# Layer 0's T1, M and output-bias products as three passes of split operands, and one load ring for x and transposed y

## What is computed

```python
q = Wq y + bq;  k = Wk y + bk;  v = Wv x + bv          # 8 heads of 32 channels
attn = softmax((q kT) / sqrt(256))                     # per head, 32 x 32
o = Wo (attn v) + bo + x
x1 = groupnorm over all channels and positions of o
```

## Time and profile before

| | |
|---|---|
| median of 3 runs | 1543.38 us (1541.15 to 1543.43) |
| the profiled execution | 1542.93 us, its span 1541.1 us |
| PE busy | 1511.2 us, 98% of the span |
| DVE busy | 1278.6 us, 83% |
| ACT busy | 1108.9 us, 72% |
| POOL busy | 450.8 us, 29% |
| granted TensorE clock, mean | 0.995 |

### The profile page before, as it was taken

The page is one execution under the profiler, slowest core; times in us unless marked ns, Lnnn a source line. Parts: engine busy times, 40 slices in busy tenths (PEclk is TensorE's granted clock), DMA queues, the critical chain, the costliest instruction groups (busy, mean ns, idle before and its releaser), DMA issues.

```text
span 1541.1 us, 54826 instructions
## 1 busy us (share of the span) xinstructions
PE 1511.2 (98%) x24146; PEld 1274.8 (83%) x24146; DVE 1278.6 (83%) x2024; ACT 1108.9 (72%) x2064; POOL 450.8 (29%) x294
## 2 busy tenths in 40 slices
PE   9999999999999999999999999999999999999995
PEld 6888888888888888888888888888888888888883
DVE  5778888888788887978879888888888889788897
ACT  6667676777767777677776776867767776777765
POOL 1114133141331413314142141422314133141321
PEclk9999999999999999999999999999999999999998
DMA  7232331423315233142422414233142331524212
GB/s 250 56 99 83 111 124 38 152 84 118 111 36 152 84 118 111 54 148 71 143 86 84 132 57 145 84 111 121 55 151 78 120 116 41 149 83 129 59 49 91
DMA packets 96397, 157.28 MB, mean 102 GB/s; under 512 B 5408, under 2 KB 38304, under 8 KB 96032
## 3 DMA queue, kind: packets, MB, share of 16 engines
q1 hardware_dynamic: 96160, 153.78, 31.8%
HBM read 120.20 MB, written 33.55 MB: 100 GB/s over the span
## 4 chain that ended last, share of the span: by engine, by line
PE 96%; DVE 1%; ACT 1%; issue 1%; POOL 0%; ACTq 0%; POOLq 0%; DVEq 0%
PE pj_ps L313 46%; PE l_ps L313 12%; PE s_ps L328 9%; PE w_ps L339 8%; PE l_ps L424 7%; PE w_ps L357 7%; PE l_ps L441 2%; PE l_ps L468 2%; PE l_ps L462 1%; PE l_ps L471 1%; PE s_ps L499 0%; PE l_ps L450 0%; DVE o_sb L972 0%; PE l_ps L432 0%; PE l_ps L489 0%
## 5 line engine op out<-in xcount | busy, mean ns | idle before, releaser
L1132 POOL TENSOR_TENSOR prob<-prob,row_inv 128x1024 f32<-128x1024 f32 x128 | 257.9, 2015 | 890.4 <-DVE row_inv L864 890.4
L671 ACT CAST att_hi<-w_ps 128x256 fp32r<-128x256 f32 x256 | 83.2, 380 | 192.2 <-PE w_ps L357 192.1
L313 PE MATMUL pj_ps<-y_hi,w_hi 128*128 128x512 f32 x510 | 207.4, 407 | 0.0
L313 PE MATMUL pj_ps<-y_hi,w_lo 128*128 128x512 f32 x510 | 202.0, 396 | 0.0
L313 PE MATMUL pj_ps<-y_lo,w_hi 128*128 128x512 f32 x510 | 202.0, 396 | 0.0
L859 DVE TENSOR_REDUCE row_sum<-prob 128x16 f32<-128x1024 f32 x128 | 155.0, 1211 | 49.2 <-ACT prob L640 49.1
L847 DVE TENSOR_REDUCE row_max<-s_ps 128x16 f32<-128x1024 f32 x128 | 155.6, 1215 | 21.2 <-PE s_ps L328 21.2
L328 PEld LDWEIGHTS s_ps<-k_s,q_s 32*64 32x64 f32 x8192 | 130.8, 133 | 43.1 <-issue 35.2
L1149 POOL TENSOR_TENSOR o_sb<-o_sb,u_sb 128x1024 f32<-128x1024 f32 x60 | 157.7, 2638 | 0.9
L854 DVE TENSOR_TENSOR prob<-s_ps,row_max 128x1024 f32<-128x1024 f32 x128 | 155.6, 1215 | 0.1
L635 ACT COPY prob_t<-w_ps 128x512 f32<-128x512 f32 x256 | 152.2, 596 | 3.8 <-PE w_ps L339 3.1
(11 more groups left out here) (139 smaller groups left out, 3552.2 us busy)
## 6 DMA issues: line engine op xcount, KB each, us to landing
y_raw<-in_ctx SPq DMA_DIRECT2D x64, 512.0 KB, 4.9
yt_raw<-in_ctx_t SPq DMA_DIRECT2D x64, 512.0 KB, 4.6
x_raw<-in_x SPq DMA_DIRECT2D x64, 512.0 KB, 5.1
out_z<-o_sb SPq DMA_DIRECT2D x60, 512.0 KB, 3.6
mask_b<-in_mask SPq DMA_DIRECT2D x64, 256.0 KB, 4.0
out_z<-o_sb SPq DMA_DIRECT2D x8, 256.0 KB, 2.7
u_sb<-in_w SPq DMA_DIRECT2D x2, 512.0 KB, 5.8
w_sb<-in_w SPq DMA_DIRECT2D x1, 1024.0 KB, 10.7
```

The source lines that it names most:

```text
L313: last = mm(dst, lhs, rhs, start=i == 0, stop=i == len(todo) - 1)
L1132: nc.gpsimd.tensor_tensor(cut, cut, row_inv[:, u % 2, :].unsqueeze(2).to_broadcast([P, 2 * HEADS, CHUNK]), ALU.mult).then_inc(probs_done, 1)
```

## The change

- Wk and Wv of layer 0 are split once into fp32r pairs (`w0_hi`, `w0_lo`), and bv into `bv_hl`. Wv is loaded into a part of u_sb. The ACT copies stand ahead of its loop, the DVE subtractions (`weights_low`) in slot 3 of the first sample.
- The Gram matrix is split in each sample: on ACT in slot 6 `split_upper` (two copies, 128x256 and 128x128) directly behind `copy_att`, and `split_lower` in the place of `copy_lower`; on DVE `gram_low` (three subtractions, 128x256, 128x128, 128x128) directly behind `sum_y`, which now signals `gram_done`.
- T1 is 2 x 2 three-pass products: 12 PE instructions of 256 columns in the place of 8.
- U is split: the ACT copy in slot 10 writes u_hi, and DVE's new `u0_low` (one 128x512 subtraction, slot 10, behind `split_y`) writes u_lo and signals `u0_copied`.
- M is 12 PE instructions of 256 columns in the place of 8, the bias product 8 of 2 columns in the place of 8 of 1; DVE adds the bias in two steps.
- Transposed y and x share two buffers. `load_yt` of the next sample's first two blocks moves to slots 14 and 15, `load_x` of the first two to slots 3 and 4.

```diff
-                if exists(n, 4, q - 2):
+                if q >= 4:
+                    sp.wait_ge(x_hi_done, count(n, 4, q - 2))
+                    sp.wait_ge(x_lo_done, count(n, 4, q - 2))
+                elif q >= 2:
                     sp.wait_ge(yt_hi_done, count(n, 4, q - 2))
...
-                    for start, load in ((S_SPLIT_T + 1, load_yt), (S_X + 1, load_x)):
...
+                    if s in (1, 2):
+                        load_yt(n, s + 1)
+                    if s in (3, 4):
+                        load_x(n, s - 3)
+                    if s - (S_X if last else S_X + 1) in (0, 1):
+                        load_x(n, s - (S_X if last else S_X + 1) + 2)
+                    if s in (14, 15) and not last:
+                        load_yt(n, s - 10)
@@ PE @@
                     for i in range(HALVES):
-                        for k in range(HALVES):
-                            last = mm(l0_ps[1][:, i * E:(i + 1) * E], gram[:, k, i * P:(i + 1) * P], w0_sb[:, K_W, k, :], start=k == 0, stop=k == 1)
+                        cut = slice(i * P, (i + 1) * P)
+                        last = three_pass(l0_ps[1][:, i * E:(i + 1) * E],
+                                          [((g_hi[:, k, cut], g_lo[:, k, cut]), (w0_hi[:, K0_SPLIT, k, :], w0_lo[:, K0_SPLIT, k, :])) for k in range(HALVES)])
...
                     for k in range(HALVES):
+                        cut = slice(k * P, (k + 1) * P)
+                        three_pass(l0_ps[0][:, k * E:(k + 1) * E],
+                                   [((w0_hi[:, V0_SPLIT, i, cut], w0_lo[:, V0_SPLIT, i, cut]), (u_hi[:, i, :], u_lo[:, i, :])) for i in range(HALVES)])
+                    for k in range(HALVES):
+                        cut = slice(k * P, (k + 1) * P)
                         for i in range(HALVES):
...
+                            mm(l0_ps[1][:, 2 * k:2 * k + 2], u_hi[:, i, cut], bv_hl[:, i, :], start=i == 0, stop=False)
+                            last = mm(l0_ps[1][:, 2 * k:2 * k + 2], u_lo[:, i, cut], bv_hl[:, i, :], start=False, stop=i == 1)
@@ ACT @@
+            def split_upper(n):
+                act.wait_ge(upper_done, count(n, 1, 0))
+                for i in range(HALVES):
+                    copy(g_hi[:, i, i * P:], gram[:, i, i * P:])
+
+            def split_lower(n):
                 act.wait_ge(lower_ready, count(n, 1, 0))
-                copy(gram[:, 1, 0:P], l0_ps[0][:, E:E + P]).then_inc(gram_done, 1)
+                copy(g_hi[:, 1, 0:P], l0_ps[0][:, E:E + P]).then_inc(gram_hi_done, 1)
...
                         copy_att(n, u - LAG)
+                    if s == S_SUM:
+                        split_upper(n)
                     if not first and s in (4, 6):
                         group_normed(n - 1, s // 2)
@@ DVE @@
+            def gram_low(n):
+                dve.wait_ge(gram_hi_done, count(n, 1, 0))
+                for i in range(HALVES):
+                    tt(g_lo[:, i, i * P:], gram[:, i, i * P:], g_hi[:, i, i * P:], ALU.subtract)
+                tt(g_lo[:, 1, 0:P], l0_ps[0][:, E:E + P], g_hi[:, 1, 0:P], ALU.subtract).then_inc(gram_done, 1)
+
+            def u0_low(n):
+                dve.wait_ge(u0_hi_done, count(n, 1, 0))
+                tt(u_lo[:, :, :], l0_ps[1][:, :].rearrange("p (i o) -> p i o", i=HALVES), u_hi[:, :, :], ALU.subtract).then_inc(u0_copied, 1)
...
                     if s == S_SUM:
                         sum_y(n)
+                        gram_low(n)
+                    if first and s == 3:
+                        weights_low()
...
+                    if s == S_U:
+                        u0_low(n)
```

More of the change, by code:

```diff
@@ L42 @@
 Q_W, K_W, V_W, O_W = range(4)
+Q0, K0, O0 = range(3)
+K0_SPLIT, V0_SPLIT = range(2)
 C_IDENT, C_HEAD, C_RESID, C_MEAN, C_NEG = 0, P, 2 * P, 2 * P + 2 * E, 3 * P + 2 * E
@@ L73, in build @@
         mean_mat = cst[:, C_MEAN:C_MEAN + P]
-        w0_sb = sb("w0_sb", [P, 4, HALVES, E])
+        w0_sb = sb("w0_sb", [P, 3, HALVES, E])
+        w0_hi = sb("w0_hi", [P, 2, HALVES, E], F32R)
+        w0_lo = sb("w0_lo", [P, 2, HALVES, E], F32R)
+        bv_hl = sb("bv_hl", [P, HALVES, 2], F32R)
         w1_hi = sb("w1_hi", [P, 4, HALVES, E], F32R)
@@ L121, in build @@
         o_bias = sb("o_bias", [P, HALVES])
+        o_part = sb("o_part", [P, HALVES])
+        g_hi, g_lo, u_hi, u_lo = m_hi, m_lo, m_hi, m_lo
         o_sb = sb("o_sb", [P, HALVES, L])
@@ L230, in load_x @@
             def load_x(n, q):
-                if exists(n, 4, q - 2):
+                if q >= 2:
                     sp.wait_ge(x_hi_done, count(n, 4, q - 2))
-                if exists(n, 4, q - 2):
                     sp.wait_ge(x_lo_done, count(n, 4, q - 2))
+                else:
+                    sp.wait_ge(yt_hi_done, count(n, 4, q + 2))
+                    sp.wait_ge(yt_lo_done, count(n, 4, q + 2))
                 sp.dma_start(x_raw[:, q % 2], x_d[n + q // 4][:, :, (q % 4) * BT:(q % 4 + 1) * BT]).then_inc(x_in[q % 2], 16)
@@ L449, in layer0 @@
                                 o = i * P + DH * h
-                                mm(l0_ps[0][DH * h:DH * h + DH, P + i * DH:P + (i + 1) * DH], y_sum_b[:, k, :], w0_sb[:, K_W, k, o:o + DH],
+                                mm(l0_ps[0][DH * h:DH * h + DH, P + i * DH:P + (i + 1) * DH], y_sum_b[:, k, :], w0_sb[:, K0, k, o:o + DH],
                                    start=k == 0, stop=k == 1)
@@ L455, in layer0 @@
                                 o = i * P + DH * h
-                                last = mm(l0_ps[0][DH * h:DH * h + DH, i * DH:(i + 1) * DH], w0_sb[:, Q_W, k, o:o + DH], t1[:, k, o:o + DH],
+                                last = mm(l0_ps[0][DH * h:DH * h + DH, i * DH:(i + 1) * DH], w0_sb[:, Q0, k, o:o + DH], t1[:, k, o:o + DH],
                                           start=k == 0, stop=k == 1)
@@ L461, in layer0 @@
                     for i in range(HALVES):
-                        last = mm(l0_ps[1][:, i * E:(i + 1) * E], a0_wide[:, i, :], w0_sb[:, O_W, i, :], start=True, stop=True)
+                        last = mm(l0_ps[1][:, i * E:(i + 1) * E], a0_wide[:, i, :], w0_sb[:, O0, i, :], start=True, stop=True)
                     last.then_inc(u0_ready, 1)
@@ L735, in _ @@
             last.then_inc(consts_done, 1)
+            copy(w0_hi[:, K0_SPLIT], w0_sb[:, K0])
+            copy(w0_hi[:, V0_SPLIT].rearrange("p h o -> p (h o)"), w_raw[:, 2 * W_HALF:2 * W_HALF + HALVES * E])
+            copy(bv_hl[:, :, 0:1], col[:, V_BV0, :].unsqueeze(2)).then_inc(w0_hi_done, 1)
             def body(n, first, last):
@@ L915, in layer0 @@
                     tt(m_lo[:, :, :], m_t[:, :, :], m_hi[:, :, :], ALU.subtract).then_inc(m_lo_done, 1)
-                    tt(o_bias[:, :], l0_ps[1][:, 0:HALVES], col[:, V_BO0, :], ALU.add).then_inc(o_bias_done, 1)
+                    parts = l0_ps[1][:, 0:2 * HALVES].rearrange("p (k a) -> p k a", a=2)
+                    tt(o_part[:, :], parts[:, :, 0], col[:, V_BO0, :], ALU.add).then_inc(bias_step, 1)
+                    dve.wait_ge(bias_step, count(n, 1, 0))
+                    tt(o_bias[:, :], parts[:, :, 1], o_part[:, :], ALU.add).then_inc(o_bias_done, 1)
                 elif S_MX <= s < S_MX + BLOCKS:
```

38 lines of the change are left out of this document (21 added, 17 removed).

## The result

| | before | after |
|---|---|---|
| median (range) | 1542.27 us (1541.06 to 1543.43) | 1564.07 us (1559.26 to 1567.58) |
| ratio, 95% interval | | 1.0139 [1.0106, 1.0172] |
| span of the profiled execution | 1541.1 us | 1557.4 us |
| PE, DVE, ACT busy | 1511.2, 1278.6, 1108.9 us | 1513.4, 1318.6, 1120.2 us |

The change makes the kernel slower by 1.4%. The forecast was +0.7%, with the right sign, and the delay that it describes came as described; but 1564.07 is 9.2 us above the forecast of 1554.9 and outside of its range, 1544 to 1562. First, the page of after: its busy times (the answer to the earlier trace rows), and the shares of the chain that ended last.

A forecast was written before the change was run, and what follows sets the result against it. PE bounds the kernel, with DVE arriving together at slot 8. Thirteen steady samples at +0.88 (+11.4), samples 3 and 4 -0.2 and -0.6, first +0.7, last +0.2: +11.5 on the span, 1554.9 us at the median, range 1550 to 1562 (1544 including B, D).

The forecast's parts named there:

- PE's own gains: On PE, T1 and M each gain 0.3 us per sample at 0.12 per instruction; bias product unchanged; 9.6 over 16.
- rival D: On PE, the bias product gets cheap, 0.6 us per sample or 9.6: 1545, no change; chance 0.08.
- The rule on fast weight load: On PE's bias product, rounded-type loads about twice as fast; would lose 0.4 us per sample; not adopted, rows show equal loads.
- The delay: Slots 6 to 8: join +0.5, DVE +1.24, PE's transposes +1.18; less T1's or M's 0.3, +0.88 per steady sample.
- Rivals A: At slot 8, PE decides alone and all DVE work is hidden: -9.6 + 1.3 gives 1535; chance 0.12.
- B: On POOL, the join isn't delayed; only gram_low's 0.74 counts: +0.38 per sample, 1548.3; chance 0.18.
- Rival C: New PE pauses in slots 7 and 8 bring the clock down in each sample: 25 us more, 1580; chance 0.08.
- the pauses of samples 3 and 4: At slot 8 PE is late by itself in these samples, so the delay is hidden: -0.2 and -0.6.
- the first sample: Ahead of yt_hl, weights_low costs 1.3 us once; less 0.6 of PE's gains, +0.7.
- The tail: In the last sample DVE is behind at M: +0.2.
- The second failed term: From profile to median: the median taken as 0.45 above the profiled execution, 1554.4 becoming 1554.9.

The follow-up runs named there:

- before_pad_shift_64: Kernel before, with 64 more PE instructions ahead of the loop and 16 more (four small products) in each sample: 1543.67 us, ratio 1.0019.
- act_copies: Kernel before, with two ACT copies of the Gram matrix's upper part added ahead of group_normed, nothing on DVE or PE: 1549.81 us, ratio 1.0054.
- dve_time: Kernel before, with three unused DVE reductions (about 0.74 us) added behind y_sum_b, nothing else: 1549.47 us, ratio 1.0053.
- shift_64: Changed kernel, with 19 tiny products at the start of PE's stream (64 more PE instructions): 1551.85 us, ratio 1.0072 to before.
- after_again: Changed kernel run once more, no edit: 1560.72 us, ratio 1.0141 to the kernel before.
- branch_first_shift_64: Changed kernel, split_upper behind group_normed, z's statistics in slot 6, y_lo behind slot 7's branch, 64 more PE instructions at the start: 1527.47 us, ratio 0.9913.
- early_stats_late_upper: Changed kernel, split_upper moved behind group_normed and z's two statistics instructions moved ahead of y_sum_b in slot 6: 1544.82 us, ratio 1.0023 to before.

## Why the prediction was right, and where it failed

**PE's own gains: right.** T1's twelve start 0.12 us apart. M runs from 839.60 to 841.01, 1.41 us, as worked out. The eight bias instructions take 0.81 us up to the next start (841.01 to 841.82), as in the kernel before (835.62 to 836.43), neither cheaper (rival D) nor dearer: the loads of L492 take 192 ns, as in the earlier trace rows. The rule on fast weight load that the prediction quoted from the Trainium skill (page TensorE: Matmul & The Clock Gate, section Weight-path perf modes) would have loads of the rounded type faster than plain ones; no row here agrees.

**The delay: right in size and place.** Join +0.50 (forecast 0.5), y_lo +1.24 (+1.24), att_lo of slot 8 +1.23 (+1.24), PE's transposes +1.23 (+1.18), clean sample +0.86 to +0.90 (+0.88; 94.49 against before_pad's 94.13 less its 0.54 is +0.90). Rivals A and B are out, and act_copies and dve_time show the two halves by themselves, 0.45 and 0.66 us a sample. There was some luck in this: y_sum_b came 0.03 us behind the join, so 0.03 us more of delay could have let it in first, a case that no run shows. The order on POOL and DVE agrees with what the Trainium skill says of the shared port pair (page SBUF — State Buffer, section Who interferes with whom): the small copy takes as long as the join does. Rival C, a fall of the clock in each sample, didn't come: in after the granted clock is 1.00 from 20 to 1540 us, so that even the one fall of before is gone.

**The failed step: the pauses of samples 3 and 4.** Of the 9.2 us missed, 4.8 lie in the profiled span and 4.4 in the step from it to the median, below. The sum on the span was +11.5 and +16.3 came. By parts: the start of y_sum_b in the first sample +0.98, the rest of that sample 0, samples 1 to 14 +13.5, the last sample from y_sum_b on +1.7. The forecast had +0.7 for the first sample in all, 12 x 0.88 - 0.8 = +9.8 for samples 1 to 14, and +1.1 for the last. Thus 3.8 of the 4.8 us missing lie in samples 1 to 14. There the prediction took PE's pauses in samples 3 and 4 to be a property of these samples that would return and hide the delay; that is 2 x 0.88 + 0.8 = 2.6 us. Before the change PE's transposes of slot 8 came 12.18 and 13.99 us behind y_sum_b's start in these two samples, for 10.83 in the others; after it they come at 12.06 in all. DVE and PE of sample 4, before and then after:

```profile
429.92 1.92 DVE L929 COPY y_sum_b<-y_sum 128x64 f32<-128x64 f32 x1
443.91 0.60 PE L339 MATMUL w_ps<-cst,prob 128*128 128x128 f32 x4
```

```profile
432.36 2.42 DVE L980 COPY y_sum_b<-y_sum 128x64 f32<-128x64 f32 x1
444.42 0.63 PE L354 MATMUL w_ps<-cst,prob 128*128 128x128 f32 x4 [0.21 <-DVE att_lo L902]
```

Those pauses follow instruction transfers, at places set by PE's instruction count. The change adds 16 PE instructions to a sample, the pauses moved to slots 10 to 12 and 14 to 0, and hid nothing; with 10.9 us for 9.5 they added 1.4. The prediction had looked at slot 8 alone: there only these two samples differ, but from one y_sum_b to the next the samples of before take 93.63 to 97.42 us, and nine of fifteen are over 0.05 above the shortest. Its sum had no term for what such pauses would be in the new kernel.

**The tail** was short by 0.6 us in after, by 0.2 with the stray pauses away (from the sixteenth y_sum_b to the end 76.66 us in shift_64, 75.87 in before_pad_shift_64 with 0.54 of its own; both have a fall of the granted clock there).

**The second failed term: from the profile to the median.** The prediction took over the 0.45 us by which the median of before lay above its profiled execution. It was 4.8 in the first runs, 1.1 in after_again, whose median of 1560.7 lies inside of the range. What those executions did is not recorded, so the cause stays open. Kernels with little stray time repeat to 2.5 us (shift_64, before_pad_shift_64, branch_first_shift_64), those with much differ by up to 9 (early_stats_late_upper 1541.26 to 1550.55); that fits transfers that come at other times in each execution, but isn't shown.

**What the change costs by itself.** Without stray pauses in either, shift_64 against before_pad_shift_64 less 16 x 0.54 = 8.6: 1551.85 - 1535.0 = +16.8 us by the medians (+16.1 against the kernel before beside each, 1541.5 and 1540.7), 1548.8 - 1533.6 = +15.2 by the spans, all with 0.8 us of shift_64's later start. The forecast, even without its error on samples 3 and 4, was 14.1.

**Open** is what makes a transfer start late in one sample and not in the next. In after those with long pauses had started 12.8 to 13.5 us behind the one before, but some as late had no pause.

## What to carry over

Where two engines arrive together, look for what is added to the one that seems idle, or to a third that releases it: here it was paid in full (0.66 and 0.45 us a sample); look for held instructions, such as y_sum_b, and put useful work into that time. A pause with no releaser inside a dense burst of small PE instructions may be a wait for the next 16 KB of instructions: here it moved when the instruction count moved, so don't carry it from one kernel's profile to another's, compare kernels by segments free of it, and try some 64 instructions more ahead of the loop before judging an edit worth less than 1%.

## What was not expected of the hardware

PE seems to run out of instructions: in all 186 pauses it goes on 1.4 us (1.2 to 2.3) after a 16 KB transfer has landed, it is idle for up to 1.7 us at a time, and by the stream's place alone the stray time of 14 samples is 1.4, 8.9 or 19.8 us, with 4.8 of the last due to the lower clock behind the longest pauses. The Trainium skill (page Runtime: NRT & Kernel Launch, section Instruction fetch mechanics) has the same blocks of 16 KiB with 256 instructions, and calls the cost of crossing one "mostly hidden". For these bursts the runs disagree: the same work took 1551.85 or 1568.31 us.
